# An expert loop whose first bias is added by TensorE and whose f16 half comes from ScalarE

## The reference

```
logits = tokens @ router_w.T;  probs = softmax(logits);  the best 2 of 8 experts, weights renormalised
for e in range(8):
    h = gelu(tokens @ w1[e] + b1[e])        # w1: 8 x 256 x 256,  b1: 8 x 256
    y = h @ w2[e] + b2[e]                   # w2: 8 x 256 x 256
    out = out + combine[:, e:e+1] * y
```

## Time and profile before

| | us |
|---|---|
| median of 3 executions | 2443.84 (2440.5 to 2450.08) |
| the profiled execution, its own time | 2460.1 |
| its span in the trace | 2458.3 |
| MoE 0 dispatch, from its first instruction to VectorE's last | 1353.2 to 1475.8 |
| MoE 0 experts, first transposes to the last scatter | 1483.2 to 1650.7 |
| MoE 1 experts | about 2020 to 2417 |

### The profile page before, as it was taken

The page is one execution under the profiler, slowest core; times in us unless marked ns, Lnnn a source line. Parts: engine busy times, 40 slices in busy tenths (PEclk is TensorE's granted clock), DMA queues, the critical chain, the costliest instruction groups (busy, mean ns, idle before and its releaser), DMA issues. The chain is left out here.

```text
span 2458.3 us, 84235 instructions
## 1 busy us (share of the span) xinstructions
PE 2004.6 (82%) x28694; PEld 1522.9 (62%) x28695; DVE 2066.0 (84%) x3804; ACT 1751.1 (71%) x2771; POOL 635.1 (26%) x604
## 2 busy tenths in 40 slices
PE   6649999999999999999996307865897209999995
PEld 3327666666666666666665205652586209999995
DVE  5879999999999999999997746768798547888883
ACT  5669999999999999999994524546687426666662
POOL 3431111111111111111110463440164642333331
PEclk9869999999999999999998558995898559999997
DMA  2013232323232323232332233434022452223235
GB/s 82 1 34 91 74 89 73 90 73 90 72 91 72 91 71 91 71 92 71 92 89 73 83 126 116 116 93 146 30 69 76 160 177 46 49 47 49 50 49 152
DMA packets 296697, 203.12 MB, mean 83 GB/s; under 512 B 153587, under 2 KB 277958, under 8 KB 296358
## 3 DMA queue, kind: packets, MB, share of 16 engines
q1 hardware_dynamic: 275840, 163.70, 24.5%
q0 software_dynamic: 19776, 35.73, 5.6%
q10 hardware_dynamic: 998, 2.62, 0.3%
HBM read 64.79 MB, written 112.92 MB: 72 GB/s over the span
## 5 line engine op out<-in xcount | busy, mean ns | idle before, releaser
L595 DVE TENSOR_TENSOR plow<-prob 128x1024 f16<-128x1024 f32 (+1 forms) x1024 | 1128.1, 1173 | 4.7 <-ACT prob L506 4.7
L506 ACT ACTIVATE prob<-scores 128x1024 f32<-128x1024 f32 x1024 | 998.9, 1026 | 91.3 <-PE scores L638 63.6
L658 PEld LDWEIGHTS outp<-vs,prob 128*128 128x128 bf16 x7680 | 516.1, 98 | 277.9 <-issue 215.8
L658 PE MATMUL outp<-vs,prob 128*128 (+1 forms) x7680 | 604.2, 193 | 27.2 <-DVE plow L595 16.5
L638 PE MATMUL scores<-qT,kT 128*128 (+1 forms) x2048 | 611.6, 380 | 7.6 <-DMA kT<-shift_rows 2.7
L660 PE MATMUL outp<-vs,plow 128*128 (+1 forms) x7680 | 601.6, 193 | 0.0
L660 PEld LDWEIGHTS outp<-vs,plow 128*128 128x128 f16 x7680 | 503.3, 97 | 59.8 <-issue 0.6
L448 POOL TENSOR_TENSOR osum<-osb 128x128 f32<-128x128 f32 x64 | 85.8, 1341 | 968.3 <-DVE rec L600 968.3
L1527 POOL DMA_INDIRECT token_sums<-m1eyo,m1edest x71 | 132.4, 1864 | 292.9 <-DMA token_sums<-m1eyo,m1edest 183.6
L1370 PE MATMUL m1eph<-m1exT,m1ew1c 128*128 128x128 f16 x3408 | 204.3, 220 | 1.7 <-issue 1.7
L1370 PEld LDWEIGHTS m1eph<-m1exT,m1ew1c 128*128 128x128 f16 x3408 | 195.4, 99 | 2.4 <-ACT m1exT L1407 1.9
(11 more groups left out here) (398 smaller groups left out, 3375.2 us busy)
## 6 DMA issues: line engine op xcount, KB each, us to landing
sorted_rows<-zero SPq DMA_DIRECT2D x128, 522.0 KB, 5.0
staged<-qk SPq DMA_DIRECT2D x73, 128.0 KB, 2.3
m0exr<-sorted_rows SPq DMA_DIRECT2D x71, 130.5 KB
m1exr<-sorted_rows SPq DMA_DIRECT2D x71, 130.5 KB, 2.5
ls_got<-expert_rows SPq DMA_DIRECT2D x8, 1024.0 KB, 5.7
na_staged<-in_L_ffn_W_dram SPq DMA_DIRECT2D x16, 512.0 KB, 3.7
m1dstg<-in_L_ffn_W_dram SPq DMA_DIRECT2D x16, 512.0 KB
tok<-in_x_dram SPq DMA_DIRECT2D x8, 512.0 KB, 8.2
```

Of the source, the lines that this page charges most:

```text
L506: act.activation(prob[g % PBUF][:, :], scores[g % 2][:, :], ACT.Exp, scale=1.0 / (QK_SCALE * QK_SCALE)).then_inc(prob_ready, 1)
L595: dve.tensor_tensor(l[:, 0:n], p[:, 0:n], high(p)[:, 0:n], ALU.subtract).then_inc(low_ready, 1)
L658: pe.matmul(to, high(prob[g % PBUF])[:, cols], v, start=(g == 0 and i == 0 and j == 0), stop=False, skip_group_check=True)
```

## The change

It is made under `narrow = NF < 4`, which holds for MoE 0 and not for MoE 1. The bias b1 is loaded as 8 rows of 256, split in a high and a low f16 half by ScalarE and VectorE, and two DMAs put the halves into rows 0 and 32 of a fifth block of 256 columns behind each expert's w1 (GpSimd has cleared that block). The copy w1c is then 1280 columns in place of 1024. TensorE ends each group of six matmuls with a seventh, the bias block against a tile of ones. ScalarE makes both gelus of a tile, to f32 and to f16, each over 256 columns without a bias; the cast on VectorE is gone, and so are the copy b1c and two waits of `halve`. In both mixtures `rows_out` takes the expert's number from one of four registers that `aim` filled, and has no register load.

```diff
@@ dispatch @@
-            sp.dma_start(b1n[:, :], b1_dram.rearrange("e (n p) -> (e n) p", p=P)).then_inc(b_in, 16)
+            sp.dma_start(b1n[:, :], b1_dram if narrow else b1_dram.rearrange("e (n p) -> (e n) p", p=P)).then_inc(b_in, 16)
             for i, (src, hi, lo, width) in enumerate(parts):
                 if i >= 3:
                     sp.wait_ge(w_split, i - 2)
                 sp.dma_start(wide(i), src).then_inc(w_in[i % 3], 16)
+                if narrow and i == NP // 2:
+                    sp.wait_ge(b_cleared, 1)
+                    sp.wait_ge(b_high, 1)
+                    sp.dma_start(b1t[0:1, :, :], b1h[:, :]).then_inc(b_placed, 16)
+                    sp.wait_ge(b_taken, 1)
+                    sp.dma_start(b1t[LOW_ROW:LOW_ROW + 1, :, :], b1l[:, :]).then_inc(b_placed, 16)
...
-                if t == 1:
+                if t == G and narrow:
+                    dve.wait_ge(b_high, 1)
+                    dve.scalar_tensor_tensor(out=b1l[:, :], in0=b1n[:, :], scalar=W_SCALE, in1=b1h[:, :], op0=ALU.mult,
+                                             op1=ALU.subtract).then_inc(b_taken, 1)
+                if t == 1 and not narrow:
...
+                if t == G - 1 and narrow:
+                    act.wait_ge(b_in, 16)
+                    act.activation(b1h[:, :], b1n[:, :], ACT.Copy, scale=W_SCALE).then_inc(b_high, 1)
...
+            if narrow:
+                pool.memset(b1t[:, :, :], 0.0).then_inc(b_cleared, 1)
@@ experts, tensor @@
+                        if narrow:
+                            last = pe.matmul(ph[(u * NQ + j) % 4][:, h * ET:(h + 1) * ET],
+                                             w1c[u % 2][:, 2 * KB, f * P:(f + 1) * P], ones[:, 0:ET],
+                                             start=False, stop=True)
@@ experts, scalar @@
-                act.wait_ge(aimed, i + 1 + NX)
+                act.wait_ge(y_ready if narrow else aimed, i + 1 + (0 if narrow else NX))
...
+                    if narrow:
+                        both = ph[b][:, 0:2 * ET].rearrange("p (h s) -> p h s", h=2)
+                        act.activation(hf[b][:, :, :], both, ACT.Gelu, scale=1.0 / W_SCALE)
+                        act.activation(hh[u % 2][:, 2 * j:2 * j + 2, :], both, ACT.Gelu, scale=1.0 / W_SCALE
+                                       ).then_inc(act_ready, 1)
+                        continue
@@ experts, vector @@
-                e = expert_of(dve, reg, i)
+                e = expert_of(dve, regs[u % 4], i)
...
-                dve.tensor_copy(b1c[u % NR][:, :], b1t[:, ds(e, 1), :].squeeze(1))
+                if not narrow:
+                    dve.tensor_copy(b1c[u % NR][:, :], b1t[:, ds(e, 1), :].squeeze(1))
...
-                dve.wait_ge(y_ready, i + 1)
+                if not narrow:
+                    dve.wait_ge(y_ready, i + 1)
                 for j in range(NQ + 1):
                     if j < NQ:
                         dve.wait_ge(act_ready, i * NQ + j + 5)
+                    if j < NQ and not narrow:
                         dve.tensor_copy(hh[u % 2][:, 2 * j:2 * j + 2, :], hf[(u * NQ + j) % 4][:, :, :]
                                         ).then_inc(hh_ready, 1)
...
-                e = expert_of(dve, y_reg, i)
+                e = the_expert(dve, regs[u % 4])
```

More of the change, by code:

```diff
@@ L882, in dispatch @@
     NF = F // P
+    narrow = NF < 4
+    LOW_ROW = 32
     NX = 4
@@ L897, in dispatch @@
         bias = sb("bias", [P, E_N])
-        b1n = sb("b1n", [E_N * NF, P])
+        b1n = sb("b1n", [E_N, F] if narrow else [E_N * NF, P])
+        b1h, b1l = [sb(n, [E_N, F], F16) for n in ("b1h", "b1l")] if narrow else (None, None)
         xn = [sb(f"xn{u}", [P, D]) for u in range(NX)]
@@ L935, in dispatch @@
         b_in = sem("b_in")
+        b_cleared = sem("b_cleared")
+        b_high = sem("b_high")
+        b_placed = sem("b_placed")
         sums_begun = sem("sums_begun")
@@ L991, in _ @@
                                  ).then_inc(sums_begun, 16)
+            if narrow:
+                sp.wait_ge(b_placed, 32)
             if sums_dram is not None:
@@ L1261, in experts @@
 def experts(nc, name, F, w1, w2, b1t, b2_dram, sorted_dram, y_dram, tile_expert, tile_row, tile_code, room,
-            ident16):
+            ident16, ones):
     NF = F // P
     NQ = NF // 2
-    NX = NY = NR if NF < 4 else 2
+    narrow = NF < 4
+    WROWS = w1.shape[2]
+    NX = NY = NR if narrow else 2
     U = 2 * NR
@@ L1277, in experts @@
         xT = [sb(f"xT{u}", [P, 2 * KB, ET], F16) for u in range(2)]
-        b1c = [sb(f"b1c{u}", [P, NF], F32) for u in range(NR)]
-        w1c = [sb(f"w1c{u}", [P, 2, KB, F], F16) for u in range(2)]
+        b1c = None if narrow else [sb(f"b1c{u}", [P, NF], F32) for u in range(NR)]
+        w1c = [sb(f"w1c{u}", [P, WROWS, F], F16) for u in range(2)]
         dest = [sb(f"dest{u}", [P, 1], I32) for u in range(U)]
@@ L1370, in first @@
                                 last = pe.matmul(ph[(u * NQ + j) % 4][:, h * ET:(h + 1) * ET],
-                                                 w1c[u % 2][:, w, k, f * P:(f + 1) * P], xT[u % 2][:, x, :],
-                                                 start=(k6 == 0), stop=(k6 == 3 * KB - 1))
+                                                 w1c[u % 2][:, w * KB + k, f * P:(f + 1) * P], xT[u % 2][:, x, :],
+                                                 start=(k6 == 0), stop=(k6 == 3 * KB - 1 and not narrow))
                                 k6 += 1
+                        if narrow:
+                            last = pe.matmul(ph[(u * NQ + j) % 4][:, h * ET:(h + 1) * ET],
+                                             w1c[u % 2][:, 2 * KB, f * P:(f + 1) * P], ones[:, 0:ET],
+                                             start=False, stop=True)
                     last.then_inc(h_ready, 1)
@@ L1446, in _ @@
         def _(dve):
-            reg = dve.alloc_register(name + "dve_expert")
-            y_reg = dve.alloc_register(name + "dve_y_expert")
+            regs = [dve.alloc_register(f"{name}dve_expert{j}") for j in range(4)]
             def aim(i, u, it):
-                e = expert_of(dve, reg, i)
+                e = expert_of(dve, regs[u % 4], i)
                 if not isinstance(i, int) or i >= 2:
                     dve.wait_ge(h_ready, i * NQ - NQ)
-                dve.tensor_copy(w1c[u % 2][:, :, :, :], w1[:, ds(e, 1)].squeeze(1)).then_inc(w1_ready, 1)
+                dve.tensor_copy(w1c[u % 2][:, :, :], w1[:, ds(e, 1)].squeeze(1)).then_inc(w1_ready, 1)
                 dve.wait_ge(x_in[u % NX], uses(it, u, NX) * 16 + 16)
                 tail = xr[u % NX][:, D:RW]
-                dve.tensor_copy(b1c[u % NR][:, :], b1t[:, ds(e, 1), :].squeeze(1))
+                if not narrow:
+                    dve.tensor_copy(b1c[u % NR][:, :], b1t[:, ds(e, 1), :].squeeze(1))
                 if summed:
@@ L1477, in halve @@
                         k = j - 1
-                        dve.wait_ge(hh_ready, i * NQ + k + 1)
+                        if not narrow:
+                            dve.wait_ge(hh_ready, i * NQ + k + 1)
                         dve.tensor_tensor(hl[u % 2][:, 2 * k:2 * k + 2, :], hf[(u * NQ + k) % 4][:, :, :],
@@ L1601, in moe @@
         tile_code = sb2("tile_code", [P, MAXT])
-        w1_halves = sb2("w1", [P, E_N, 2, KB, F], F16) if w1_split is None else w1_split
+        narrow = F // P < 4
+        w1_rows = sb2("w1", [P, E_N, 2 * KB + narrow, F], F16) if w1_split is None else \
+            w1_split[:, :, :, :, :].rearrange("p e h k f -> p e (h k) f")
+        w1_halves = w1_rows[:, :, 0:2 * KB, :].rearrange("p e (h k) f -> p e h k f", k=KB)
         w2_halves = sb2("w2", [P, 2, E_N, F // P, D], F16)
-        b1t = sb2("b1t", [P, E_N, F // P])
+        b1t = w1_rows[:, :, 2 * KB, :] if narrow else sb2("b1t", [P, E_N, F // P])
         dispatch(nc, name + "d", tok, stats, F, by_probs, add_norm, gate, gate_by_expert, gate_bias,
@@ L1607, in moe @@
                  tile_row, tile_code, sorted_dram, y_dram if out_dram is not None else None, ident16, ident32)
-        experts(nc, name + "e", F, w1_halves, w2_halves, b1t, b2, sorted_dram, y_dram, tile_expert, tile_row,
-                tile_code, tok if out_dram is not None else None, ident16)
+        experts(nc, name + "e", F, w1_rows, w2_halves, b1t, b2, sorted_dram, y_dram, tile_expert, tile_row,
+                tile_code, tok if out_dram is not None else None, ident16, consts[1])
     if out_dram is not None:
```

5 lines of the change are left out of this document (3 added, 2 removed).

## The result

| | us | ratio to before |
|---|---|---|
| before, in the same set of runs | 2442.97 (2440.5 to 2450.08) | |
| after | 2404.02 (2401.92 to 2407.15) | 0.984 [0.9823, 0.9857] |
| the profiled execution after, own time and span | 2403.46, 2401.7 | |

The account below looks back on a forecast made before the run. VectorE's order of work, idle included, was taken to bound MoE 0's loop, a late-gelu chain afterwards. Looped tiles -17.8, other tiles -1.7, dispatch +0.5 gave -19.0 us from the median 2443.84: 2425 us, range 2408 to 2440.

Parts of the forecast that it names:

- The second register load, -0.19 in the mean: MoE 0's loop, VectorE: dropping the load ahead of yo saves 0.19 us a tile in the mean, 0.16 late in the body.
- VectorE's own order: MoE 0's loop: VectorE's work and idle places set the step, 2.307 us in the mean, 1.79 after the change.
- the extra idle there (+0.04): MoE 0's loop: 0.04 us added to the step for steps early in the body, where yo to w1c is 0.86.
- Late gelus in 6 of 8 tiles: MoE 0's loop, ScalarE: 6 of 8 tiles have a late gelu and a 2.00 us step, 2 run at 1.79.
- the gelu comes promptly: Rival, MoE 0's loop: VectorE's 1.79 or TensorE's 1.66 decides; gain 33 to 42 us, 2402 to 2411; chance 0.15.
- the forecast's step of 1.99: MoE 0's loop: mean step after the change, 1.95 us plus 0.04, gaining 0.317 on each of 56 looped tiles.
- the late chain: MoE 0's loop: two-step chain from w1c through matmuls, late gelu, hl and yo to w1c; 3.99 us, 2.00 a step.
- the floor of 1.66: MoE 0's loop: TensorE's whole work a tile after the change, 18 matmuls of 128 columns and 6 of 256, 1.66 us.
- the gelu pair 0.66: MoE 0's loop, ScalarE: two gelus of 256 columns without bias take 0.66 us together, +0.03; 0.85 from above.
- ScalarE as the bound: Rival, MoE 0's loop: late gelus are ScalarE's own pace, step 2.28 us, nothing won; 2436 to 2445; chance 0.22.
- Slower: Rival, MoE 0's loop: ScalarE's pace with the gelu pair at 0.85, step 2.47 us; 13 us more, 2457; chance 0.05.
- The register load was not the idle: Rival, MoE 0's loop: VectorE has 1.98 in the mean, late chain 2.08; gain about 13 us, 2431; inside forecast's band.

Follow-up runs that it names:

- the preload: Kernel after with VectorE's one register load made one tile ahead, between dest and hl: 2443.62 us against 2472.84, ratio 0.9882; again 2444.47 against 2473.64, ratio 0.9895.

## Why the forecast was wrong, by its steps

The direction was right, and of the size half was found. Two steps failed.

**The second register load, -0.19 in the mean: it is -0.45.** I took the idle in front of yo for the whole price. Without the load yo starts before hl has ended, and yo to w1c early in the body shortens as well. VectorE's own order is then 2.307 - 0.33 - 0.45 = 1.53 and not 1.79, and falls under TensorE's 1.66. The experiment with one load shows the sum, 2.307 to 1.860; the kernel with the load ahead of `halve` and the two with neighbouring loads show that it is the load, and no wait, that VectorE stands for. Why w1c early in the body comes sooner without it is not shown. I had left the extra idle there (+0.04) in place. (The reading that the early steps alone lift the mean by 0.17 over 2.14 was short of a term: the step in which the loop branches back takes 2.57 before, 0.05 of the 0.17.)

The Trainium skill ("Runtime: NRT & Kernel Launch", section on instruction fetch) gives some 200 ns for loading a register from HBM; here the table is on the chip, and the rows show 0.31 for the first load and none for its neighbour, so the row decides and that figure would have misled in the same direction as mine.

**Late gelus in 6 of 8 tiles, taken as the kernel's own.** In prompt surroundings none is late, with either kernel, so "the gelu comes promptly" (2402 to 2411, chance 0.15) is what happened, and 2404.02 lies in it. That is luck in part: its bounds were VectorE's 1.79, which carries the load's wrong size, and TensorE's 1.66, and the 1.739 between them has the branch in it. The reason that I gave it, the pointer or the replaced wait, was wrong: the kernel without a pointer has late gelus in late surroundings, the kernel before with a third load has none in prompt ones. The error had a mark that I saw and dismissed: the profiled execution lay 16 us above the median, and I wrote that the loop's waits do not scale with that. They belong to the same surroundings as those 16 us.

In late surroundings both steps can be told apart: of the 0.25 by which the forecast's step of 1.99 is over the 1.739, 0.11 is left there (1.99 against 1.878), and 0.14 goes with the surroundings. With the measured 0.34 for hl to yo and 0.58 for yo to w1c, the late chain is 0.60 + 1.50 + 0.66 + 0.09 + 0.34 + 0.58 = 3.77, or 1.89 a step; the kernel after has 1.878 there. That they agree to 0.01 is chance, for not every gelu is late by as much and the branch adds 0.05 a step; but the chain was the right view; two of its terms were too long, 0.46 and 0.65, for the load's sake, and my mean step of 1.99 with them. The kernel gains 22 us there and E 165.1 - 138.1 = 27, so that even there 19 was a little low. In the two profiled executions (the kernel before again and the kernel after again) the other way go 5.6 us between the last scatter and MoE 1's dispatch and 2.1 in that dispatch; no run shows whether that is more than chance.

**What bounds it in the prompt case.** VectorE's own order, 0.41 + 0.19 + 0.34 + 0.58 = 1.52 with a shortest dest to hl of 0.19, is under TensorE's 1.66. So where nothing pauses the step is TensorE's: 1552.22 - 1550.57 = 1.65 from one w1c to the next, 2.11 in the step of the branch, 1.739 in the mean. This holds for about half of the steps, by the count of starts and by the run without the seventh matmul. The two-step chain with a prompt gelu and the measured terms is as long, 0.60 + 1.03 + 0.66 + 0.09 + 0.34 + 0.58 = 3.30 or 1.65 a step, so that little was left to gain behind TensorE. The forecast named the floor of 1.66 and gave it as the rival's lower end.

**Where the 36 us of E come from** (each with the one before in place): load 27.7 (26.3 counted from the 164.4), bias by TensorE 1.5, then both gelus on ScalarE 136.6 - 129.9 = 6.7. The shares hold for this order alone; taken last, the load is worth 10.9. With narrow gelus and their pointers the same move costs 1.1, so it paid only with the wide gelus, which the bias on TensorE allows. In medians the three are 28.5, 2.2 and 9.5 us, the last one across two sets of prompt surroundings.

**Terms that held.** Cast -0.33 in VectorE's order, w1c +0.07 (494 against 428 ns), w1c to dest 0.41, the gelu pair 0.66 (1552.27 to 1552.93), its start 1.03 behind the matmuls, TensorE +0.11, MoE 1 unchanged. The first scatter stands 0.9 later behind the dispatch's start than before (25.4 against 24.5), where 0.5 was forecast.
On the gelu, the Trainium skill ("VectorE: DVE Perf Modes", section on the TRN2 errata) stood against the change with a pair of 0.84. The rows show 0.66: two gelus of 385 and 379 ns, 0.28 apart. On the columns the trace agrees with the page: without a pointer, 128 columns take 275 ns and 256 take 385, 0.11 more. What the 0.84 leaves out is that the pointer goes as well, which gives back 0.09 for each gelu (364 against 275); 0.84 - 0.18 = 0.66. The forecast's rows at 475 and 384 had shown as much.

**Rivals that fell.** ScalarE as the bound (2436 to 2445, 0.22): in the prompt case it is busy for 13.21 of 18.5 us, and even with late gelus the step is 1.878, not 2.28. Slower (0.05): the pair is 0.66, under the 0.69 from which that rival would decide. "The register load was not the idle": it was, and more.

## What to carry to other kernels

A stall in the profile is not its price: compare start to start of the same two instructions with and without it, for neighbours overlap when nothing stands between them (0.22 of idle, 0.31 of time, 0.45 of step). When the profiled execution lies off the median, ask first which of the waits belong to that difference, and work out the change once with and once without them. A high busy share of an engine whose ends are modelled is no proof of a bound: count its starts in the step (18.28 and 18.05 of 18.5 went with steps of 1.87). Register loads go side by side, or into one with its value kept in a register for later: the second beside a first costs nothing, one in another place costs again, unless the engine stands waiting there anyway, as in the preload.

## What was unexpected of the hardware

- The same kernel has two sets of surroundings. Before: 2443 to 2445 or 2467 to 2474; after: 2404 or 2445. In the long ones both dispatches take 131 to 140 and 136 to 141 us in place of 123 to 124 and 125 to 127, and a gelu starts up to 0.5 us later behind its matmuls. The mean granted clock hardly differs (0.905 and 0.903 for the kernel after). It is not the chip alone: one chip appeared in sets of both kinds. Late gelus cost the kernel before nothing (E 164.4 without, 165.1 with), and the kernel after 8.2 (129.9 and 138.1). The cause stays open.
- A register load on VectorE costs some 0.3 us where it stands (0.31 ahead of yo, 0.27 ahead of the cast, 0.30 ahead of w1c), 0.45 and 0.32 of the whole step in the first two places, and nothing beside another or where VectorE waits for a gelu. On TensorE, ahead of the transposes, it costs 1.892 - 1.739 = 0.15 a step.
- A bias pointer costs a gelu of 128 columns 0.09 us (364 against 275 ns), almost as much as 128 more columns (385 against 275).
- The step in which the loop branches back is some 0.4 us longer, once a pass: on VectorE yo to w1c is 0.99 against 0.58, and TensorE pauses for 0.31 ahead of its transposes and 0.09 behind them.
